# A second router by chunks: regions of rows per expert, sent as each chunk is routed, and shared tail tiles behind the experts

## The chip, the cores and the metric

One core of one Trainium2 chip runs the kernel. Its engines are named as in the profile: PE (TensorE, with PEld its weight loads), DVE (VectorE), ACT (ScalarE), POOL (GpSimd), SP (SyncE), and 16 DMA engines. The metric is the device time of one execution in microseconds; the median of three executions of the kernel before is 945.3 us (945.02 to 947.12).

## The reference, cut to what matters

Two layers over 2048 tokens of width 256, float32. The first layer (causal attention with 16 heads, and a mixture of 16 experts, two per token) is not touched, but for zeros that are written beside it. The second:

```python
xn = _layernorm(x)
x = x + _L1_attn_ref(xn, W, b) + _L1_ffn_ref(xn, ...)

# attention without a softmax, from sums over the tokens
q, k, v = split(xn @ W + b)
attn = q / norm(q, axis=1) * sum(k / norm(k, axis=1) * v, axis=1)

# 4 of 16 experts per token, and a shared expert
probs = softmax(xt @ w_router)
top_w, top_i = top_k(probs, 4);  top_w = top_w / sum(top_w)
moe_out = sum over the 4 of top_w * (silu(xt @ we1[e]) * (xt @ we3[e])) @ we2[e]
shared = silu(xt @ ws1) * (xt @ ws3) @ ws2
out = shared / 5 + moe_out * 4 / 5
```

## The kernel before, in words

Tokens lie in 16 tiles of 128 (T), in four chunks of four tiles (C, TC). Each engine has its own program in each of three blocks; semaphores order them, and a block ends when all engines have ended theirs.

`stage_first` is the first layer: an order of steps planned in advance (`attention_plan`) for PE, ACT, DVE and POOL. SP's program in it also writes zeros over `xd1`, the scratch for the second layer's dispatched rows, in five transfers (line 723).

`stage_second` has two parts. Its front is a loop over tiles (DVE's turns from line 1690, PE's from 1815): PE transposes the attention's output, DVE divides by the softmax sums, PE transposes back and multiplies by `w_o` (1840), DVE adds to the residual (1695) and takes norm statistics. After every four tiles DVE makes the variance (1702), ACT its root (1635), DVE the normalized rows `xn` one chunk behind. `turn_and_score(c)` on PE (1799) transposes a chunk of `xn`, ACT copies it to `xt` (1642; two tiles ahead of the next chunk's root, two behind it), and PE computes router logits (1811). The calls for chunks 0, 1 and 2 stand in PE's turns 9, 13 and 17; the last follows the loop. Then PE forms the Gram product of `xn` (1851), from which the norms and sums of the linear attention follow, runs 16 units of the shared expert's first layer (`shared`, 1863 and 1869; ACT's silu, DVE's `gated`, 1739), with the norms' work after 13 of them, and multiplies ten "tail" tiles: the shared expert's second layer and `q`'s projection (1910, 1912). DVE adds them in pairs (1793). In the meantime DVE routes all 16 tiles at once: softmax (1721 to 1727), four best per token and their indices (`route_best`, 130), then `route` (140): masks, ranks by two matmuls on PE (`route_ranks`, after Gram tile 8), a scan of counts, a slot for each row so that an expert's rows lie together and padded to 128, and the table `tile_e` with each tile's expert. `route` hands each of the four choices to POOL, which sends 64 times 128 rows of 1032 bytes to `xd1` by indirect DMA (1625). A row carries its own place for the way back.

`stage_experts` runs 79 tiles of 128 dispatched rows through their experts, in a loop unrolled 16 times (`rolled`, 1268): SP loads a tile at `j * 128` (1356), PE transposes it (1475), multiplies by both first matrices (1484), transposes the product (1492), multiplies by the second (1499); ACT and DVE copy and gate; POOL computes the rows' home (1448) and scatters the result by indirect DMA (1454). PE's program loads 20 registers with expert numbers at the head of each body. Then PE multiplies the last six tail tiles (1509), SP and ACT each fetch eight tiles' four rows per token (1363, 1390), and the weighted sums are made by DVE for tiles 0 to 7 (1430) and by PE for tiles 8 to 15, with diagonal matrices of weights that DVE has built (1422, 1517); DVE adds what PE has summed (1438), and SP stores tile by tile (1366).

## Time and profile before

| | |
|---|---|
| median of three executions | 945.3 us |
| profiled execution, its own time | 946.62 us |
| its span | 944.6 us, granted clock 0.964 |
| busy in the span | PE 864.8 (92%), DVE 642.2 (68%), ACT 417.2 (44%), POOL 422.0 (45%) |
| DMA moved | 113.6 MB, mean 120 GB/s |

```profile
PE   5887789899999999999999977789998879999997
DVE  5589799888788888887888952575714514444466
POOL 3323065515544336435353464000477826766640
PEclk9998599999999999999999999896999989999999
DMA  9643956421561312911110122640122225555549
```

Each digit is the busy share of a fortieth of the span (23.6 us) in tenths, for PEclk the clock granted to TensorE in tenths of full speed. The attention fills the first 25 slices. The second layer's block begins with slice 26 (about 598 us), the expert loop with slice 33 (about 770 us), and the last slice and a half is the fetch and the sums. POOL idles in slices 27 and 28, and the dispatch of rows lies in slices 29 to 33.

### The profile page before, as it was taken

To read this page: it belongs to the slowest core of one execution; us is meant where nothing else is said; L and a number is where in the kernel's file an instruction comes from. 1 tells how busy PE (TensorE), PEld (TensorE's weight loads), DVE (VectorE), ACT (ScalarE), POOL (GpSimd) and SP (SyncE) were. 2 spreads that over 40 slices of the span, in tenths; PEclk is the share of its full clock that TensorE was granted. 3 is DMA by queue.
4 is the path that set the end of the run, shared out by engine and by line. 5 is a ranking of instruction groups with operands and counts; after the bars stand their busy time and mean duration, and the time that the engine had idled before them with its cause. 6 is when DMAs were issued, how large, how long until landed. Compare 5 with 4: busy or idle time off the path is not lost. (4 is left out here: it accounts for less than half of the span.)

```text
span 944.6 us, 16014 instructions
## 1 busy us (share of the span) xinstructions
PE 864.8 (92%) x4827; PEld 468.3 (50%) x4828; DVE 642.2 (68%) x1528; ACT 417.2 (44%) x739; POOL 422.0 (45%) x719
## 2 busy tenths in 40 slices
PE   5887789899999999999999977789998879999997
PEld 3533223334444444444444321567544667787886
DVE  5589799888788888887888952575714514444466
ACT  3633145465666666665666667222112013333310
POOL 3323065515544336435353464000477826766640
PEclk9998599999999999999999999896999989999999
DMA  9643956421561312911110122640122225555549
GB/s 330 210 131 120 217 113 174 143 45 34 123 176 61 115 46 78 204 45 52 43 50 23 57 66 65 234 162 1 51 100 97 81 76 147 156 152 155 153 164 359
DMA packets 71393, 113.60 MB, mean 120 GB/s; under 512 B 12054, under 2 KB 55318, under 8 KB 70806
## 3 DMA queue, kind: packets, MB, share of 16 engines
q1 hardware_dynamic: 50774, 57.76, 22.2%
q0 software_dynamic: 16000, 45.70, 14.3%
q10 hardware_dynamic: 4544, 9.21, 3.2%
q8 instruction: 38, 0.62, 0.3%
q14 instruction: 37, 0.30, 0.1%
HBM read 58.19 MB, written 54.15 MB: 119 GB/s over the span
## 5 line engine op out<-in xcount | busy, mean ns | idle before, releaser
L1069 DVE TENSOR_REDUCE part_max<-ps_row 128x1 f32<-128x512 f32 (+3 forms) x560 | 353.5, 670 | 69.8 <-PE ps_row L1223 40.5
L939 ACT ACTIVATE probs<-ps_st 128x1024 f32<-128x1024 f32 (+3 forms) x320 | 278.5, 897 | 201.1 <-PE ps_st L1202 199.9
L1127 PE MATMUL ps_o<-probs,v_all 128*17 128x512 f32 (+3 forms) x1280 | 148.5, 536 | 14.4 <-ACT probs L939 8.6
L1223 PE MATMUL ps_row<-ks,qs 96*128 96x512 bf16 (+3 forms) x320 | 109.6, 376 | 12.2 <-DVE part_max L1069 9.0
L1223 PE MATMUL ps_row<-xt_ks,qs 96*128 96x512 bf16 (+3 forms) x320 | 103.1, 350 | 1.0 <-DVE part_max L1069 0.5
L1454 POOL DMA_INDIRECT yd<-moe_ys,moe_home x79 | 78.1, 989 | 44.2 <-POOL moe_home L1448 28.8
L1202 PE MATMUL ps_st<-qs,ks 99*128 99x512 bf16 (+3 forms) x320 | 88.8, 360 | 3.7 <-DMA qs<-max_parts 3.5
L1202 PE MATMUL ps_st<-qs,xt_ks 99*128 99x512 bf16 (+3 forms) x320 | 82.7, 348 | 2.1 <-ACT probs L939 1.3
L1484 PE MATMUL moe_ps_h<-w,moe_xs_t 128*128 x316 | 83.3, 387 | 0.0
L1223 PEld LDWEIGHTS ps_row<-ks,qs 96*128 96x128 bf16 x320 | 31.9, 100 | 94.3 <-DVE part_max L1069 57.3
L1401 DVE TENSOR_TENSOR moe_hid<-moe_ps_h,moe_act 128x128 f32<-128x128 f32 x79 | 23.0, 291 | 76.8 <-ACT moe_act L1384 76.8
L1625 POOL DMA_INDIRECT xd<-xn,slot x64 | 65.9, 1030 | 18.7 <-issue 9.8
L811 POOL TENSOR_SCALAR_AFFINE_SELECT probs<-probs 128x256 f32<-128x256 f32 x128 | 52.4, 416 | 48.9 <-ACT probs L939 47.5
L821 POOL TENSOR_SCALAR moe_h_tanh<-moe_h_tanh 128x128 f32<-128x128 f32 x47 | 24.9, 529 | 96.9 <-ACT moe_h_copy L951 96.6
L1223 PEld LDWEIGHTS ps_row<-xt_ks,qs 96*128 96x128 bf16 x320 | 30.8, 96 | 74.2 <-DVE part_max L1069 40.7
L1377 ACT COPY moe_xs_t<-moe_ps_x 128x256 f32<-128x256 f32 x79 | 29.4, 373 | 76.1 <-PE moe_ps_x L1475 75.8
L1484 PEld LDWEIGHTS moe_ps_h<-w,moe_xs_t 128*128 128x128 f32 x316 | 55.0, 194 | 4.6
L799 POOL DMA_INDIRECT xd<-o_t,slot x32 | 31.3, 977 | 47.3 <-ACT probs L939 42.8
L1127 PEld LDWEIGHTS ps_o<-probs,v_all 128*17 128x17 f32 x1280 | 21.8, 95 | 61.1 <-ACT probs L939 37.1
L1226 PE MATMUL ps_row<-mask,ident 128*128 128x128 bf16 x256 | 50.7, 225 | 0.0
L1202 PEld LDWEIGHTS ps_st<-qs,xt_ks 99*128 99x128 bf16 x320 | 27.4, 98 | 41.9 <-ACT probs L939 21.7
L1499 PE MATMUL moe_ps_y<-we,moe_hid_t 128*128 x158 | 47.2, 382 | 0.0
(266 smaller groups left out, 1329.4 us busy)
## 6 DMA issues: line engine op xcount, KB each, us to landing
moe_xs<-xd SPq DMA_DIRECT2D x79, 129.0 KB, 2.1
xd<-zeros SPq DMA_DIRECT2D x4, 2064.0 KB, 10.3
qk_parts<-probs SPq DMA_DIRECT2D x16, 384.0 KB, 3.3
qs<-qk_parts SPq DMA_DIRECT2D x96, 64.0 KB, 2.5
moe_xs<-xd POOLq DMA_DIRECT2D x47, 128.0 KB, 2.4
yd<-moe_ys POOLq DMA_DIRECT2D x47, 128.0 KB, 2.1
xd<-zeros POOLq DMA_DIRECT2D x2, 2048.0 KB, 15.6
moe_w<-in_w ACTq DMA_DIRECT2D x2, 2048.0 KB, 20.1
```

The lines of the kernel that those rows point to most:

```text
L799: pool.indirect_dma_start(out=m.xd0, out_offset=bass.IndirectOffsetOnAxis(m.r["slot"][:, choice, i:i + 1], 0), in_=m.xn[:, i, :], in_offse ...
L811: pool.affine_select(out=corner, in_=corner, compare_op=ALU.is_ge, fill=keep, base=0, pattern=[[0, 2], [1, P]], channel_multiplier=-1).the ...
L939: act.activation(probs[:, at % NPB, :, off:CH], ps_st[at % 2][:, :, off:CH], ACT.Exp, scale=HD ** -0.5).then_inc(exp_done, 1)
L1069: dve.tensor_reduce(part_max[reduced % 2][:, h:h + k, i, j:j + 1], bank[:, 0:k * w].rearrange("p (h w) -> p h w", h=k), AX_X, ALU.max).the ...
L1127: mm = pe.matmul(ps_o[32 * q:32 * q + HD + 1, off:CH], m.v_all[:, k, g * HG + q, :], probs[:, (at + q // 2) % NPB, q % 2, off:CH], start=F ...
L1202: mm = pe.matmul(ps_st[n % 2][:, h, off:CH], ks[g % 2][:, q, k * P:(k + 1) * P], qs[c][:, q, off:CH], start=True, stop=True)
L1223: mm = pe.matmul(cols, qs[c][0:KROWS, h, i * P:(i + 1) * P], ks[g % 2][0:KROWS, h, j * CH:j * CH + w], start=True, stop=(j < c))
L1226: mm = pe.matmul(cols[:, w - P:w], m.ident16[:, :], m.mask16[:, :], start=False, stop=True)
L1454: pool.indirect_dma_start(out=yd, out_offset=bass.IndirectOffsetOnAxis(home[:, k:k + 1].bitcast(U32), 0), in_=ys[:, k % U, :], in_offset=N ...
L1484: mm = pe.matmul(ps_h[b][:, :], xs_t[:, b, k, :], w1[:, k, bass.ds(e, 1), :], start=(k == 0), stop=(k == KH - 1))
L1499: pe.matmul(ps_y[b][:, :], hid_t[:, b, :], w2[:, bass.ds(e, 1), :], start=True, stop=True).then_inc(y_done, 1)
L1625: pool.indirect_dma_start(out=m.xd1, in_=xn[:, i, :], in_offset=None, out_offset=bass.IndirectOffsetOnAxis(r["slot"][:, k, i:i + 1], 0)).t ...
```

## The change

It alters where the second layer routes, where rows go, and who makes the last sums.

- **Routing by chunks.** The logits, the softmax, the best four, the masks, the ranks and the slots are computed for a chunk of four tiles at a time (`chunk_ranks`, `chunk_best`, `chunk_slots`). Those of chunks 0 and 1 stand between DVE's turns in the loop over tiles: scores of 0 after turn 10, best of 0 after 12, slots of 0 after 13, scores of 1 after 14, best of 1 after 16; the rest follows the loop. PE multiplies for the ranks of chunks 0 and 1 behind `turn_and_score(1)` and `(2)`, for 2 and 3 behind Gram tiles 0 and 5. ACT's exp is four steps.
- **A region per expert.** Expert `e` owns rows from `e * CAP` on, `CAP` = 2048 + 128, so a row's slot needs only the counts of the chunks before. `xd1` grows to 16 * 2176 + 128 rows. POOL sends a chunk's 16 tiles-of-choices as its slots are ready, waiting for the landing of a half's rows before it overwrites the home column.
- **Pads.** Zeros are written over one tile only (the last); when all is routed, SP copies it behind the end of each region, 16 transfers.
- **A table of first rows** (`tile_row`), made by `tile_tables` beside `tile_e` in pieces between gated units. SP loads 16 of its entries into registers for every 16 tiles.
- **Tail.** `TAIL_FIRST` 10 becomes 2: fourteen tail tiles are multiplied behind the experts. DVE makes all weighted sums, two tiles at a time, and SP stores pairs. Diagonals and PE's sums are gone.

```diff
-        if "home" not in r:
-            dve.tensor_copy(r["slot"][:, k, :], r["slotf"][:, k, :]).then_inc(slots_ready, 1)
-        else:
-            ...
+        dve.tensor_copy(r["slot"][:, k, :], r["slotf"][:, k, :]).then_inc(slots_ready, 1)
...
+def chunk_ranks(pe, r, c, masks_ready):
+    pe.wait_ge(masks_ready, c + 1)
+    flat = r["any16"][:, c * TC:(c + 1) * TC, :].rearrange("p i e -> p (i e)")
+    pe.matmul(r["ps_ranks"][c], r["before16"][:, :], flat, start=True, stop=True)
+    return pe.matmul(r["ps_counts"][c], r["ones16"][:, :], flat, start=True, stop=True)
+
+def chunk_best(dve, step, r, c, scores, masks_ready):
+    tiles = range(c * TC, (c + 1) * TC)
+    cs = slice(c * TC, (c + 1) * TC)
+    route_best(dve, step, r, scores, tiles)
+    step.then(dve.tensor_copy(r["argf"][:, cs, 0:TOP1], r["arg"][:, cs, 0:TOP1]))
+    step.then(dve.tensor_tensor(r["hots"][c], r["argf"][:, cs, 0:TOP1].rearrange("p i k -> p k i").unsqueeze(
+        3).to_broadcast([P, TOP1, TC, E]), r["iota_e"].unsqueeze(1).to_broadcast([P, TOP1, TC, E]), ALU.is_equal))
+    ...
+        dve.tensor_reduce(r["any16"][:, cs, :], r["hots"][c].rearrange("p k i e -> p i e k"), AX_X,
+                          ALU.add).then_inc(masks_ready, 1)
+
+def chunk_slots(dve, step, r, c, ranks_ready, slots_ready):
+    given, start, place = r["given"][:, c, :, :], r["start"][:, c, :, :], r["place"]
+    dve.wait_ge(ranks_ready, c + 1)
+    step.then(dve.tensor_copy(given[:, :, 1:TC + 1], r["ps_counts"][c].rearrange("p (i e) -> p e i", e=E)))
+    step.then(dve.tensor_tensor_scan(start.rearrange("p e i -> p (e i)"), r["inside"],
+                                     given.rearrange("p e i -> p (e i)"), 0.0, ALU.mult, ALU.add))
+    step(dve.tensor_tensor(place, r["ps_ranks"][c].rearrange("p (i e) -> p i e", e=E),
+                           start[:, :, 0:TC].rearrange("p e i -> p i e"), ALU.add))
+    if c + 1 < C:
+        step(dve.tensor_copy(r["given"][:, c + 1, :, 0], start[:, :, TC]))
+    step.sync()
+    step.then(dve.tensor_tensor(r["placed"], r["hots"][c], place.unsqueeze(1).to_broadcast([P, TOP1, TC, E]),
+                                ALU.mult))
+    cs = slice(c * TC, (c + 1) * TC)
+    step.then(dve.tensor_reduce(r["slotf"][:, :, cs], r["placed"], AX_X, ALU.add))
+    dve.tensor_copy(r["slot"][:, :, cs], r["slotf"][:, :, cs]).then_inc(slots_ready, 1)
...
 stage_first, SP
-                    if c >= 2 and at_tile < NT1:
-                        clear(sp, m, m.xd1, at_tile, min(NT1, at_tile + CLEAR), m.cleared[1])
-                        at_tile += CLEAR
+                    if (g, c) == (1, 0):
+                        clear(sp, m, m.xd1, E * CAP // P, E * CAP // P + 1, m.cleared[1])
...
 stage_experts
-                    sp.dma_start(xs[:, u % U, :], xd[bass.ds(j * P, P), :]).then_inc(x_in[u % U], 16)
-            rolled(sp, 0, tiles, BODY, tick)
+                    sp.dma_start(xs[:, u % U, :], xd[bass.ds(first_rows[u], P), :]).then_inc(x_in[u % U], 16)
+            rolled(sp, 0, tiles, BODY, tick, load_rows)
...
+            for n in range(T // 2):
+                pair = (2 * n, 2 * n + 1)
+                dve.wait_ge(fetched[n], 32)
                 for k in range(top):
-                    step(dve.tensor_scalar(diag[:, t, k, :], m.ident[:, :], m.r["weight"][:, i, k:k + 1], float(TOP1 + 1),
-                                           ALU.mult, ALU.mult))
...
+                    for i in pair:
+                        step(dve.scalar_tensor_tensor(m.x[:, i, :], yg[i][:, k, :], m.r["weight"][:, i, k:k + 1],
+                                                      m.x[:, i, :], ALU.mult, ALU.add))
+                    step.sync()
+                if 2 * n < TAIL_FIRST:
+                    dve.sem_inc(finished, 1)
                 else:
+                    dve.wait_ge(tail_done, n + 1 - TAIL_FIRST // 2)
+                    both = m.x[:, 2 * n:2 * n + 2, :]
+                    dve.scalar_tensor_tensor(both, ps_tail[n].rearrange("p (i d) -> p i d", d=D), 1.0 / (TOP1 + 1), both,
                                              ALU.mult, ALU.add).then_inc(finished, 1)
...
-                    pool.tensor_tensor(home[:, j:j + 1], xs[:, j % U, D + 1:XW].bitcast(I32), ring[:, j % U:j % U + 1],
-                                       ALU.add).then_inc(home_ready, 1)
+                    pool.tensor_scalar(home[:, j:j + 1], xs[:, j % U, D + 1:XW], ring[:, j % U:j % U + 1], None,
+                                       ALU.max).then_inc(home_ready, 1)
...
-TAIL_FIRST = 10
+TAIL_FIRST = 2
-GRAM_FIRST = 8
+RANKS_IN_GRAM = {0: 2, 5: 3}
...
 stage_second, SP
+            sp.wait_ge(m.cleared[1], 16)
+            sp.wait_ge(pads_ready, 1)
+            pads = nc.values_load_multi_w_load_instructions(
+                pad_row[0:1, 0:E], engines=[mybir.EngineType.SP], ...)[1]
+            for first in pads:
+                sp.dma_start(m.xd1[bass.ds(first, P), :], m.xd1[E * CAP:E * CAP + P, :]).then_inc(padded, 16)
+            sp.wait_ge(padded, 16 * E)
...
 stage_second, POOL
+            for c in range(C):
+                pool.wait_ge(slots_ready, c + 1)
+                for k in range(TOP1):
+                    for half in range(2):
+                        i = c * TC + 2 * half
+                        if k:
+                            pool.wait_ge(dispatched[half], 32 * (c * TOP1 + k))
+                        step.then(pool.tensor_copy(xn[:, i:i + 2, DP:XW], home[:, k, i:i + 2].unsqueeze(2)))
+                        for i in (i, i + 1):
+                            pool.indirect_dma_start(out=m.xd1, in_=xn[:, i, :], in_offset=None,
+                                                    out_offset=bass.IndirectOffsetOnAxis(r["slot"][:, k, i:i + 1], 0)
+                                                    ).then_inc(dispatched[half], 16)
...
 stage_second, ACT and DVE
+                if i in (10, 14):
+                    exp_of(i // TC - 2)
...
+                if i in (10, 14):
+                    scores_of(i // TC - 2)
+                if i in (12, 16):
+                    best_of(i // TC - 3)
+                if i == 13:
+                    chunk_slots(dve, step, r, 0, ranks_ready, slots_ready)
```

## Rows read from the trace of the kernel before

**Rows 1.** Windows: length, busy PE, PEld, DVE, ACT, POOL (counts), clock, DMA share, GB/s.

```profile
300.00:400.00 100.00, 99.58 (x693) 45.67 (x695) 84.11 (x160) 62.04 (x99) 49.14 (x106) 1.00 0.44 110
...
650.00:652.00 2.00, 2.00 (x12) 2.00 (x11) 0.00 (x0) 1.73 (x3) 0.00 (x0) 0.50 0.00 0
...
908.00:945.00 37.00, 31.59 (x141) 26.32 (x141) 25.22 (x75) 0.00 (x0) 3.35 (x4) 0.99 0.78 298
```

**Rows 2.** Chain of waits that ended last: start, duration, what.

```profile
918.30 20.46 DMA we<-yd
```

**Rows 3.** Timeline of PE, second layer: start, duration, line, what [idle before <- releaser].

```profile
633.53 0.63 PE L1820 MATMUL ps_ab<-ident,o_t 128*128 128x128 f32 x4
...
648.34 2.25 PE L1806 MATMUL ps_t<-ident,xn 128*128 128x128 f32 x8
...
653.65 9.87 PE L1851 MATMUL ps_gram<-xn 128*128 128x257 f32 x36
...
679.08 1.98 PE L1869 MATMUL ps_ab<-xt,ws 128*128 128x512 f32 x4 [0.36 <-DVE o_t L1739]
...
743.04 1.89 PE L1910 MATMUL ps_gram<-ws,o_t 128*128 128x256 f32 x8
...
745.63 1.89 PE L1910 MATMUL ps_gram<-ws,o_t 128*128 128x256 f32 x8
```

**Rows 4.** Timeline of DVE, second layer: turns 14 and 17, first and last tail sums.

```profile
634.20 0.26 DVE L1684 RECIPROCAL rec<-ps_ab 128x16 f32<-128x16 f32 x1 [2.15 <-PE ps_ab L1820]
...
643.38 0.42 DVE L1695 TENSOR_TENSOR x_res<-ps_o,x_res 128x256 f32<-128x256 f32 x1 [1.56 <-PE ps_o L1840]
...
745.90 0.69 DVE L1793 SCALAR_TENSOR_TENSOR x_res<-ps_gram,x_res 128x512 f32<-128x512 f32 x1 [1.34 <-PE ps_gram L1912]
...
766.55 0.69 DVE L1793 SCALAR_TENSOR_TENSOR x_res<-ps_t,x_res 128x512 f32<-128x512 f32 x1 [4.49 <-PE ps_t L1912]
```

**Rows 5.** Timeline of POOL, the dispatch: its first, longest and last send.

```profile
670.84 1.00 POOL L1625 DMA_INDIRECT xd<-xn,slot  x1 [0.36 <-POOL xn L1623]
...
741.04 4.37 POOL L1625 DMA_INDIRECT xd<-xn,slot  x1 [0.31 <-issue]
...
760.74 0.97 POOL L1625 DMA_INDIRECT xd<-xn,slot  x1 [0.31 <-issue]
```

**Rows 6.** Groups by line, DVE, 595 to 670: busy us, mean ns, idle before.

```profile
L133 DVE MAX8 best<-scores 128x8 f32<-128x16 f32 x16 | 1.3, 160 | 0.0
...
L210 DVE TENSOR_TENSOR masks<-masks,count 128x256 f32<-128x256 f32 x2 | 1.2, 593 | 0.0
...
L181 DVE TENSOR_TENSOR_SCAN before<-within,count 128x256 f32<-128x256 f32 x1 | 0.7, 691 | 0.0
...
L161 DVE TENSOR_REDUCE top_sum<-best 128x16 f32<-128x64 f32 x1 | 0.2, 213 | 0.0
```

**Rows 7.** Timeline of ACT, second layer: a root in the front, a table load.

```profile
632.08 0.20 ACT L1635 ACTIVATE std<-var 128x4 f32<-128x4 f32 x1 [0.59 <-DVE var L1702]
...
651.02 1.28 ACT L1661 ACT_TABLE_LOAD   x1
```

**Rows 8.** Page: transfers (KB each, us to landing); groups by line: POOL's home step.

```profile
moe_xs<-xd SPq DMA_DIRECT2D x79, 129.0 KB, 2.1
...
L1448 POOL TENSOR_TENSOR moe_home<-moe_xs,moe_ring 128x1 int32<-128x1 int32 x79 | 15.4, 195 | 5.5 <-DMA moe_xs<-xd 3.1
```

**Rows 9.** Waits, 769 to 912: total us, times, longest.

```profile
PE moe_ps_x L1475 <- issue: 4.2, 4, 1.2
```

**Rows 10.** Timeline from 900 and page group: first and last sum, tail, mean.

```profile
909.41 1.89 PE L1509 MATMUL moe_ps_x<-ws,o_t 128*128 128x256 f32 x8
...
919.43 2.05 DVE L1430 SCALAR_TENSOR_TENSOR x_res<-moe_yg,weight,x_res 128x256 f32<-128x256 f32 x4 [3.13 <-DMA w<-yd]
...
940.74 0.75 DVE L1438 SCALAR_TENSOR_TENSOR x_res<-moe_ps_g,x_res 128x256 f32<-128x256 f32 x2
...
L1430 DVE SCALAR_TENSOR_TENSOR x_res<-moe_yg,weight,x_res 128x256 f32<-128x256 f32 x32 | 15.5, 483 | 4.8 <-DMA w<-yd 3.9
```

More of the change, by code:

```diff
@@ L35 @@
 XW = D + 2
+CAP = S + P
 YRING = 4
 IN_RANGE = "the routing counts from zero and takes the minimum with E - 1"
+ROW_IN_RANGE = "a region holds every token and P rows more, and the minimum with E * CAP is taken"
 EPS = 1e-5
@@ new lines, in choice_weights, with region_ends @@
+def choice_weights(dve, step, r, top, factor):
+    best = r["best"]
+    step.then(dve.tensor_reduce(r["sum"][:, :], best[:, :, 0:top], AX_X, ALU.add))
+    step.then(dve.reciprocal(r["sum"][:, :], r["sum"][:, :]))
+    step(dve.scalar_tensor_tensor(r["weight"][:, :, 0:top], best[:, :, 0:top], factor,
+                                  r["sum"][:, :].unsqueeze(2).to_broadcast([P, T, top]), ALU.mult, ALU.mult))
+def region_ends(dve, r, pads_ready):
+    dve.tensor_copy(r["pad_row"][:, :], r["start"][0:1, C - 1, :, TC]).then_inc(pads_ready, 1)
@@ L1285, in rolled, with shared_tail @@
         tick(j, j % unroll)
+def shared_tail(pe, m, bank, i):
+    cols = bank[:, i % 2 * D:(i % 2 + 1) * D]
+    for s in range(HS // P):
+        pe.matmul(cols, m.hid_s[:, s, i * P:(i + 1) * P], m.ws2[:, s, :], start=(s == 0), stop=False)
+    for k in range(KH):
+        mm = pe.matmul(cols, m.xt2[:, k, i * P:(i + 1) * P], m.wq[:, k, :], start=False, stop=(k == KH - 1))
+    return mm
 def stage_experts(nc, m, out):
@@ L1536, in stage_second @@
         home = l.sb("home", [P, TOP1, T], I32)
-        place = l.sb("place", [P, TOP1, T], I32)
+        given, start = l.sb("given", [P, C, E, TC + 1]), l.sb("start", [P, C, E, TC + 1])
+        inside, place = l.sb("inside", [P, E, TC + 1]), l.sb("place", [P, TC, E])
+        pad_row = l.sb("pad_row", [1, E], I32)
         w = l.sb("w_attn", [P, KH, 3 * D])
@@ L1636, in root_of, with exp_of @@
                                ACT.Sqrt).then_inc(std_ready, 1)
+            def exp_of(c):
+                cs = slice(c * TC, (c + 1) * TC)
+                act.wait_ge(logit_ready, c + 1)
+                act.activation(scores[:, cs, :], scores[:, cs, :], ACT.Exp).then_inc(exp_ready, 1)
             def copy_turned(c, tiles):
@@ L1659, in _ @@
             copy_turned(C - 1, range(TC))
-            act.wait_ge(logit_ready, 1)
-            act.activation(scores[:, :, :], scores[:, :, :], ACT.Exp).then_inc(exp_ready, 1)
+            exp_of(C - 2)
+            exp_of(C - 1)
             act.wait_ge(gram_done, 1)
@@ L1740, in gated @@
                                   ALU.mult).then_inc(hid_ready, 1)
-            for n in range(BEFORE_NORMS):
+            gated(0)
+            gated(1)
+            choice_weights(dve, step, r, TOP1, TOP1 / (TOP1 + 1))
+            tables = tile_tables(dve, step, r, NT1)
+            for n in range(2, BEFORE_NORMS):
+                next(tables, None)
                 gated(n)
```

201 lines of the change are left out of this document (103 added, 98 removed).

## The prediction

> **What bounds the kernel now.** I read busy times by stage first: PE is 99.6% busy in the attention, and in the last 37 us the DMA engines (0.78), PE and DVE share the load [rows 1]; in the expert loop PE stands only 4.2 us, for its own registers [rows 9]. The chain of waits then says how the end is made: PE up to the last expert tile, 20.46 us of fetching routed rows, DVE's last sums [rows 2]. Last the timelines. In the second layer's front (598 to 654) PE, DVE and ACT hand work to each other; from 653.65 PE runs nearly alone: the Gram product, the shared units, then ten tail tiles, 2.59 us apart [rows 3]; DVE adds their last pair at 766.55 [rows 4]. POOL sends rows beside this from 670.84 to 761.71 [rows 5]: 90.9 us for 64 sends, so POOL would hold the stage by itself if PE's part alone got shorter. The reader is to see three places: the front, the tail tiles, the end.
>
> **1. Eight tail tiles leave the stage.** Only the first pair stays, which DVE adds at 745.90; the fifth was added at 766.55 [rows 4]: 20.65 us less. The early routing also frees DVE, for which PE waited 0.36 us at 679.08 [rows 3]: -0.36. What is late next is POOL. It gets chunk 0 at about 639 (below); 64 sends at 90.9 - 3.4 (one send took 4.37 instead of 0.97) = 87.5 us end near 727, or 730 with such a send, against a stage end near 752. New are 24 waits for rows sent four sends before instead of sixteen; a pair of sends takes 2.7 us and the other half's pair lies between, so I take no wait. Until each costs 0.9 us the cover of 22 us hides them: 0.
>
> **2. The router by chunks costs time in the front.** Before, it lay in DVE's block beside the Gram product. Now scores of two chunks, the best of two and the slots of one stand inside the loop over tiles. Prices from the full-size steps [rows 6]: 64 elements take 0.21 us, 256 of a product 0.59, the scan of 256 takes 0.69, 16 maxima 1.3, and a dependent step starts 0.04 later. Scores of a chunk: two of 64 elements, 0.38. Best: three small steps 0.72, four maxima 0.40, four index searches (two instructions each) 0.66, a copy 0.22, a comparison and a sum over 256 elements 0.79: 2.8 us. Slots: copy 0.25, scan of 80 elements 0.36, two small steps 0.33, product 0.63, sum 0.46, cast 0.09: 2.1 us.
> Followed through the trace: scores(0) delays DVE's turn 11 by 0.4. best(0) stands ahead of turn 13, and turn 13 makes the variance that ACT's root at 632.08 waits for [rows 7]. Behind this root in ACT's queue stand the copies of two turned tiles, behind those on PE the logits of chunk 1 and the transposes at 633.53 [rows 3]. So PE is 3.2 us late there, and 0.2 more by the two rank matmuls. slots(0) waits for these and stands 2.1 us ahead of turn 14, which began at 634.20 [rows 4] and now begins near 639.3: +5.1. From there to turn 17 (643.38) scores(1) and best(1) add 3.2 and DVE's waits there, the longer of 1.56 us [rows 4], give back 1.9: +6.4. The last turn-and-score on PE (648.34, [rows 3]) had its input 0.9 us early; it now starts +5.6, and so does the Gram product: 659.2 instead of 653.65.
> Exp by chunks makes ACT load a table four times more, 1.28 us each [rows 7]. Three of the loads end before their input is there. The one ahead of exp(2) follows ACT's last copies and puts the masks of chunk 2 at about 661.5, where PE asks for them after its first Gram tile: +0.3, and +0.2 for two more pairs of rank matmuls. Sum of the part: 5.6 + 0.3 + 0.2 = +6.1. Bounds: 11.7 if nothing is absorbed (8.5 of steps added and 3.2 for the queue behind the root), 2 if PE's clock helps as in (a). I take 6.1, since the order of the queues leaves only the waits named to absorb.
> For the table loads the Trainium skill (ScalarE: Activation LUTs, What ACT_TABLE_LOAD costs) gives 2.66 us a switch, with a drain of 1.38 behind the load. In this trace an activation follows its load at once where its input is there. By the page exp(2) would be 1.4 us later and the time 944.6.
>
> **3. Tables, pads, clears.** The tile table and the new table of first rows are cut into pieces of 1.3 to 1.9 us between gated units, where DVE idles 2.7 us each time: 0, and 8 if that cover were gone. SP's 16 pad copies of 129 KB start near 670; a transfer of that size lands in 2.1 us [rows 8], so even one after the other they are done by 705: 0. The clears of 10 MB leave the attention, where PE was full while they ran (300 to 400 in [rows 1]): 0, with -1 as the other end. The one clear that stays is the size of one load: 0.
>
> **4. Expert loop.** SP has to load 16 registers before its first transfer. Nearest is PE, which stands those 4.2 us at the heads of four bodies, loading 20 each: 16/20 x 1.0 = +0.8, once. The later loads fall where SP waits between transfers (one each 1.63 us, 0.33 to issue): 0; 3.3 if none were hidden. POOL's maximum takes the place of an addition on 128x1 that took 195 ns [rows 8]. POOL's send begins 0.4 us behind this step, though in the stage before a send begins 0.28 behind a copy: it has some 0.12 us a tile to spare. 0, and +4 if the new form takes 0.17 us longer (0.05 x 79).
>
> **5. The end.** DVE summed eight tiles while PE summed eight with diagonal weights: 919.43 to 941.49 = 22.06 us, the pace of the fetches [rows 10]. Now DVE sums sixteen. A product-sum is 483 ns [rows 10], the next independent one starts 0.09 us before its end, a dependent one 0.04 after it. A pair of tiles is four times 0.394 + 0.483 + 0.04, 3.66 us. Seven pairs also add the shared tail, 0.69 us for 512 columns (as at 766.55), 0.61 of it in line: 4.27. In all 3.66 + 7 x 4.27 + 0.1 = 33.65 us: +11.6. The first pair lands as before, since the same transfers go first; the others land 2.8 us apart and are hidden. PE's fourteen tail tiles take 14 x 2.59 = 36.3 us from the end of its last expert tile, on the old times 909.41 to 945.7 [rows 10], and DVE asks for the last at 952: hidden by 6 us. The 32 diagonal weights (6.35 us on DVE) lay beside the fetch: leaving them out brings 0. The last store has 256 KB instead of 128: +0.4, between 0 and 1.
>
> **Sum.** -20.65 - 0.36 + 6.1 + 0.8 + 11.6 + 0.4 = -2.1 us. The profiled execution took 946.6 us for a span of 944.6; it would take 944.5 for 942.5. It stood 1.3 above the median of three, 945.3, and against that median I forecast 943.2.
>
> **The rivals.**
> (a) The front costs less. PE's clock is at 0.50 of its full speed (1.2 GHz) from 641 to 657 now, as at 650 in [rows 1]. If it stays at 2.4 the last turn-and-score takes 3.1 us as the first ones did instead of 5.3, and the Gram product 1.8 less: 939.2. Against it: the clock fell after PE had idled 1.95 and 0.89 us within 5 us, and it will idle more.
> (b) The other side: the front costs more. Behind best(0) PE idles some 3.4 us in one piece. If its clock falls to 1.2 GHz there, chunk 1's logits come 0.9 us later and turn 16's product 1.0, and a Gram product that is slow for 4 us more than now takes 2 us longer, with DVE's small steps longer beside POOL's sends (up to 0.19 us each at 672 to 674) by 1: the front costs 11 and the time is 948.1. It turns slower once the front costs over 10.1 us. For it speaks the length of the gap, against it that most of PE's work there waits for DVE anyway.
> (c) POOL's new form or SP's register loads hold the expert loop: +4, 947.2. Against it the spare times in 4.
> (d) The change does not do what it says: POOL still ends the stage, because each pair waits for its landing. At 1.5 us a wait it is 36 us later, at 766 instead of 752: 957. DVE can slow its sends: that at 741.04 took 4.37 us [rows 5] while DVE did one addition of 4.42 us with both operands in SBUF. The Trainium skill (SBUF — State Buffer, SBUF: two separate sides) says that such a DVE step and a GpSimd step exclude each other; the trace agrees in this one place. The other such DVE steps take under 0.75 us.
>
> **How the numbers follow.** About 0.2% (1.9 us) is what a measurement of this kernel can tell from no change. Chances: as worked out 0.5 (941 to 945.5, of it 0.3 below 943.4 and 0.2 above), (a) 0.17, (b) 0.17 (0.03 of it within 0.2%), (c) 0.12 (0.04 within), (d) 0.04. Faster 0.3 + 0.17 = 0.47, same 0.27, slower 0.26. The range reaches from (a) to (b): 939.2 to 948.2.
>
> **What would show it.** DVE's turn 14 about 5 us later, POOL's first send near 639.5, the Gram product near 659, the first tail matmul near 746, a stage ended by DVE near 752 with POOL done by 730, PE's first expert tile near 757, 1.63 us a tile, and in the end DVE without a wait for 33 us with PE's tail done before it. It would be wrong by a front that costs more than 10 or less than 3 us, by POOL ending the stage, by another pace in the loop, or by DVE waiting in the end.

## The result, and the profile after

The changed kernel takes 942.1 us (median of 11 runs, 940.3 to 947.7) where the kernel before takes 946.35 beside it (11 runs, 945.0 to 948.9): a ratio of 0.9958, with a 95% interval of 0.9945 to 0.9971. By the ratio that is 4.0 us less (4.2 between the two medians), where 2.1 were forecast, and 942.1 where 943.2 was. Here and below a ratio leaves out the runs that took over 1.5% longer than the fastest of the same kernel; beside the result there were none. The profiled execution has a span of 939.6 us (its own time is 941.45), against 944.6 before: 5.0 less.

To see where the 5.0 us lie I cut both traces at the same six places and count the first three from the second layer's first transpose on PE (597.97 before, 595.96 after):

| us | before | after | difference | forecast |
|---|---|---|---|---|
| attention and all ahead of it | 597.97 | 595.96 | -2.0 | 0 |
| Gram product starts | 55.68 | 62.60 | +6.9 | +5.6 |
| DVE's last addition of the stage ends | 169.27 | 155.25 | -14.0 | -14.9 |
| POOL's next block starts | 171.40 | 156.10 | -15.3 | -14.9 |
| from there to the first expert transpose | 2.04 | 2.83 | +0.8 | +0.8 |
| to PE's first tail matmul (the expert loop) | 138.00 | 138.77 | +0.8 | 0 |
| to DVE's first sum of routed rows | 10.02 | 9.69 | -0.3 | 0 |
| DVE's sums, first to last | 22.06 | 33.70 | +11.6 | +11.6 |
| from there to the end of the span | 3.11 | 2.55 | -0.6 | +0.4 |

(The Gram row and the DVE row lie inside the one for POOL's block and are not added.) The sum is -2.0 - 15.3 + 0.8 + 0.8 - 0.3 + 11.6 - 0.6 = -5.0.

The front on DVE, from the timeline of the kernel after; columns: start, duration, engine, line, operation, tiles, shapes, count, and in brackets the idle time before it and what ended it:

```profile
634.04 0.21 ACT L1725 ACTIVATE std<-var 128x4 f32<-128x4 f32 x1 [2.33 <-DVE var L1818]
```

```profile
633.84 0.17 DVE L1818 TENSOR_SCALAR var<-mv 128x4 f32<-128x4 f32 x1
636.02 0.23 DVE L262 COPY given<-ps_l 128x64 f32<-128x64 f32 x1 [2.02 <-PE ps_l L242]
...
638.06 0.26 DVE L1781 RECIPROCAL rec<-ps_ab 128x16 f32<-128x16 f32 x1
...
649.02 0.42 DVE L1811 TENSOR_TENSOR x_res<-ps_o,x_res 128x256 f32<-128x256 f32 x1
...
657.50 0.22 DVE L1797 TENSOR_REDUCE peak<-scores 128x4 f32<-128x64 f32 x1 [1.71 <-ACT scores L1731]
```

ACT's root now stands at 634.04, DVE still idles 2.02 us behind its variance and then makes slots (2.1 us) ahead of turn 14, which starts at 638.06 instead of 634.20 [rows 4]. Turn 17's addition (649.02) comes 7.65 us later than before, counted from the stage's start. The 1.71 us at 657.50 are the table load ahead of the third exponential; they are nearly hidden, since PE needs the masks only after its first Gram tile: DVE has them at 660.64, and PE's rank product starts at 660.70, 0.1 us behind that tile. PE's side of the same stretch, and the stage's end:

```profile
658.56 2.06 PE L1976 MATMUL ps_gram<-xn 128*128 128x257 f32 x4
...
675.06 1.45 PE L1988 MATMUL ps_ab<-xt,ws 128*128 128x512 f32 x3
...
745.00 1.97 PE L1366 MATMUL ps_gram<-ws,o_t 128*128 128x256 f32 x8 [0.94 <-DVE o_t L1856]
...
754.89 1.46 PE L1557 MATMUL moe_ps_x<-ident,moe_xs 128*128 128x128 f32 x4 [4.48 <-DMA moe_xs<-xd]
```

The first tail matmul follows at 745.00 (before 740.38) and only one pair of tiles stands before the experts. POOL, from its timeline: first and last send, and its next block.

```profile
639.05 1.01 POOL L1715 DMA_INDIRECT xd<-xn,slot  x1 [0.59 <-POOL xn L1713]
...
728.42 0.97 POOL L1715 DMA_INDIRECT xd<-xn,slot  x1 [0.30 <-issue]
752.06 0.13 POOL L1525 IOTA moe_ring_i<- 128x4 int32 x1 [22.67 <-POOLq L1606]
```

The sends end 22.67 us before the next block, which starts 0.85 us after DVE's last addition (750.52 and 0.69 long). In the trace of before the same row reads otherwise:

```profile
760.74 0.97 POOL L1625 DMA_INDIRECT xd<-xn,slot  x1 [0.31 <-issue]
769.37 0.13 POOL L1444 IOTA moe_ring<- 128x4 int32 x1 [7.66 <-POOLq L1532]
```

There POOL's next block started 7.66 us after its last send and 2.13 us after DVE's last addition [rows 4]. So POOL, not DVE, had the last word in that stage; the experiment with late routing below shows the same 7.6 us. The instructions at the end of the block, which the profile does not count as busy, say so directly (line, engine, operation, duration in ns, start in us):

```profile
L1532 POOLq COMPARE_BRANCH  x1: 46/46/46, 763.3 to 763.3; - x1
L1532 POOLq DRAIN  x1: 5382/5382/5382, 763.7 to 763.7; - x1
L1532 DVEq DRAIN  x1: 17/17/17, 767.5 to 767.5; - x1
L1532 SPq EVENT_SEMAPHORE  x1: 17/17/17, 769.3 to 769.3; - x1
```

POOL's program waits at its end for the landing of its rows. At 763.3, 2.6 us after the last send began, it is past that wait; then a drain instruction, which stands at the end of each engine's block, keeps POOL from 763.7 to 769.1. DVE's took 0.02 us and was over at 767.5, and the other engines go on at 769.3, when POOL's is over. After the change the same drain (5.30 us) begins at 731.2, 15 us before DVE is done.

The end, from the timelines of DVE and PE:

```profile
903.35 1.80 DVE L1511 SCALAR_TENSOR_TENSOR x_res<-moe_yg,weight,x_res 128x256 f32<-128x256 f32 x4 [9.06 <-DMA moe_yg<-yd]
...
932.71 3.62 DVE L1511 SCALAR_TENSOR_TENSOR x_res<-we,weight,x_res 128x256 f32<-128x256 f32 x8
936.36 0.69 DVE L1519 SCALAR_TENSOR_TENSOR x_res<-moe_ps_y,x_res 128x512 f32<-128x512 f32 x1
```

```profile
929.06 1.03 PE L1368 MATMUL moe_ps_y<-wq,xt 128*128 128x256 f32 x4
```

DVE works from 903.35 to 937.05 without a wait; PE's last tail tile is done at 930.1, 6.3 us before DVE asks for it.

### The profile page after: what moved, and what is told of

The parts are those of the page before. It is cut to its first block and busy times, and to the rows that moved or that the text cites. A ratio compares the mean times of both kernels' runs of the same rounds, so it can differ in the third digit from the quotient of the medians.

```text
span 939.6 us, 16080 instructions
## 1 busy us (share of the span) xinstructions
PE 849.5 (90%) x4769; PEld 455.7 (48%) x4770; DVE 654.9 (70%) x1551; ACT 422.8 (45%) x746; POOL 433.9 (46%) x720
## 5 line engine op out<-in xcount | busy, mean ns | idle before, releaser
L1536 POOL DMA_INDIRECT yd<-moe_ys,moe_home x79 | 82.5, 1045 | 31.4 <-POOL moe_home L1530 16.6
L1715 POOL DMA_INDIRECT xd<-xn,slot x64 | 63.5, 992 | 19.0 <-issue 9.7
```

Source lines behind the costliest of these rows:

```text
L1536: pool.indirect_dma_start(out=yd, out_offset=bass.IndirectOffsetOnAxis(home[:, k:k + 1].bitcast(U32), 0), in_=ys[:, k % U, :], in_offset=N ...
L1715: pool.indirect_dma_start(out=m.xd1, in_=xn[:, i, :], in_offset=None, out_offset=bass.IndirectOffsetOnAxis(r["slot"][:, k, i:i + 1], 0)).t ...
```

## The experiments

**Four parts taken back or moved, on one chip.** The kernel before took 946.35 us beside them (17 runs), as beside the result.

**1. The clears put back.**

```
+                    if c >= 2 and at_tile < NT1:
+                        clear(sp, m, m.unused, at_tile, min(NT1, at_tile + CLEAR), m.cleared[1])
+                        at_tile += CLEAR
```

> The changed kernel with the five clears of 10 MB put back at their old places in the attention, onto rows in DRAM that nothing reads, and with the wait for them on SP before the pads. The changed kernel stands 4.0 us below the kernel before (942.1 against 946.35), and in its profile the attention ended 2.0 us earlier. Theory A (the clears held the attention up): 2.0 us are given back, the ratio to the kernel before goes from 0.9958 to 0.998 and the second layer's first transpose moves from 595.96 back to 598. Theory B (the 2.0 us are the phase of PE's clock after one wait at 67 us, before any clear starts): the time stays at 942.1, ratio 0.9958, and the start of the second layer differs from 596 only if the matmuls at 67 us are slow again.

Measured: 943.85 us (12 runs), ratio 0.9977 (0.9963 to 0.9992). The ratio lies at the 0.998 of theory A and not at the 0.9958 of theory B, but its interval touches that of the change (0.9945 to 0.9971), so the times alone leave anything from nothing to over 3 us to the clears. The profile speaks for theory B: with the clears, the second layer began at 595.60.

```profile
66.75 1.88 PE L1246 MATMUL ps_st<-xt_ks,moe_ys 128*128 128x512 f32 x4
...
595.60 1.94 PE L1947 MATMUL ps_ab<-ident,o_t 128*128 128x128 f32 x8 [3.42 <-PEq L666]
```

The four products at 66.75 took 1.88 us, as after (66.84), where the profiled execution of before took 3.54 at 66.92: that difference stands 70 us ahead of the first clear. And the five profiled executions of this chip and of the result that have the changed kernel's attention (one of them with the clears) began the second layer at 595.60, 595.96, 597.33, 601.02 and 602.66. A difference of 2 us there, between one execution and another, says nothing of the change. All fourteen profiles sort by the four products: where they took 1.88 us the second layer began at 595.60 to 596.26 in five, with and without the clears, and at 598.54 in the sixth; where they were slower it began at 597.33 to 602.66 in eight, with both kernels. A cost of the clears of up to 2 us in the medians is not excluded.

**2. All ten tail tiles back in the stage.**

```
-TAIL_FIRST = 2
+TAIL_FIRST = 10
```

> The changed kernel with all ten tail tiles back in the stage before the experts, as in the kernel before. Theory: the stage ends 20.65 us later with DVE's last addition near 771.2, POOL done 40 us before it; the end loses four paired additions of 0.61 us (-2.4) and PE has 20.7 us less to do there. Sum +18.2: 960.3 us, 1.4% above the kernel before. Rival (the moved tiles cost again in the end, by contention of PE with DVE's sums or with the fetches): then taking them out of the end gives back more than 2.4 us, DVE's 33.7 us from first to last sum fall below 31, and the time is under 958.

Measured: 961.31 us, ratio 1.0171 (1.0158 to 1.0184), 19 us above the changed kernel. In the profile the stage ends 20.57 us later after its start, and DVE's sums last 31.78 us instead of 33.70: -1.92 for four additions, 0.48 each and not 0.61. The addition's 0.61 us show here too (950.18 to 950.79), but a pair of tiles without one then takes 3.78 us instead of 3.66, with 0.15 us of wait before the next pair. No contention shows: the moved tiles cost in the end what DVE's additions cost and nothing else.

**3. Routing behind the loop.** Scores, best choices and slots of chunks 0 and 1 follow DVE's last normalization; their ranks go into the Gram product.

```
-                if i in (10, 14):
-                    scores_of(i // TC - 2)
-                if i in (12, 16):
-                    best_of(i // TC - 3)
-                if i == 13:
-                    chunk_slots(dve, step, r, 0, ranks_ready, slots_ready)
...
-RANKS_IN_GRAM = {0: 2, 5: 3}
+RANKS_IN_GRAM = {1: (0, 1), 7: (2,), 12: (3,)}
```

> The changed kernel with the routing of chunks 0 and 1 (scores, best choices, slots, and ACT's exponentials) taken out of the loop over tiles and put behind it, their ranks on PE into the Gram product. Theory: the front gets its 6.6 us back: DVE's turn 14 at 632.2 instead of 638.06, the Gram product from 651.7 instead of 658.56. But POOL then has its first slots only near 656, and 64 sends take 90.3 us: POOL ends near 747 instead of 729.4 and, with its last landing, ends the stage at 748.5 in place of DVE, which would be done at 744 to 746. So of 6.6 us only some 2 arrive: 940.2. Rival A (the front's loss is not made by these steps but by the clock of PE): the Gram product still starts after 656 and the time is 945 or more, since POOL starts later. Rival B (POOL's sends get quicker when they lie apart from the front): the whole 6.6 us arrive, 935.5.

Measured: 951.12 us, ratio 1.0053 (1.0040 to 1.0066): 9 us slower than the change, where 2 less were expected; the expectation failed. In its profiled execution the second layer began at 602.66:

```profile
658.37 3.77 PE L1974 MATMUL ps_gram<-xn 128*128 128x257 f32 x8
...
669.63 0.20 PE L241 MATMUL ps_l<-any,before 128*128 128x64 bf16 x1 [1.10 <-DVE any L254]
...
675.11 0.20 PE L241 MATMUL ps_o<-any,before 128*128 128x64 bf16 x1 [0.83 <-DVE any L254]
```

```profile
665.42 1.01 POOL L1715 DMA_INDIRECT xd<-xn,slot  x1 [0.59 <-POOL xn L1713]
...
747.65 4.87 POOL L1715 DMA_INDIRECT xd<-xn,slot  x1 [0.30 <-issue]
...
759.70 0.97 POOL L1715 DMA_INDIRECT xd<-xn,slot  x1 [0.30 <-issue]
768.29 0.13 POOL L1525 IOTA moe_ring_i<- 128x4 int32 x1 [7.62 <-POOLq L1606]
```

```profile
747.26 4.42 DVE L1910 TENSOR_TENSOR x_res<-x_res,bq 128x4096 f32<-128x4096 f32 x1
...
753.01 0.69 DVE L1915 SCALAR_TENSOR_TENSOR x_res<-ps_gram,x_res 128x512 f32<-128x512 f32 x1 [1.34 <-PE ps_gram L1368]
```

The theory holds for the front: the Gram product starts 55.71 us after the stage's start, as before (55.68), so all 6.9 us come from these steps (with their exponentials and rank products), and none from PE's clock by itself (what the clock adds comes with the waits that they make). Of the 6.9 us, 4.2 reach DVE's last addition (151.04 us after the stage's start instead of 155.25): inside the Gram product PE now waits 1.10 and 0.83 us for masks, as its two rank rows show. What I had wrong is POOL. Its first send goes 62.76 after the stage's start; 64 sends last 95.3 us, one of them 4.87 beside DVE's addition of 4.42 over all tiles (the pair of [rows 5] again); and its next block starts 7.62 us after the last, 14.6 us after DVE's last addition at 753.70. I had put the first send some 2 us too early and the sends 5 us too short, and allowed 1.5 us for the landing where the landing and the drain take 7.6. Early routing is therefore worth far more than the trace of DVE and PE shows: it is what lets POOL be done in time.

**4. Two tiles' sums on PE.**

```
+                        for k in range(top):
+                            mm = pe.matmul(ps_tail[n][:, i % 2 * D:(i % 2 + 1) * D], diag[:, i - T + ON_PE, k, :],
+                                           yg[i][:, k, :], start=False, stop=(k == top - 1))
```

> The changed kernel with the routed sums of the last two tiles moved to PE, as products with diagonal weights into the banks of their shared tail; DVE makes the 8 diagonals (1.6 us) while the fetch runs. Theory (DVE alone sets the end, PE waits there 6.3 us): DVE's sums shrink by one pair, 3.66 us, to 30.0; PE's last pair gets 2 x 1.73 us longer and ends near 933.6, where DVE asks for it at 932.7: -3.66 + 0.9 = -2.8 to -3.3 us, 939 us. Rival (the end is already held by the fetch of rows or by the store): the last rows land late, PE waits for them, and the gain is under 1 us.

Measured: 941.43 us, ratio 0.9945 (0.9933 to 0.9958). DVE's sums last 30.49 us instead of 33.70, with one wait of 0.35 for PE:

```profile
938.03 0.69 DVE L1527 SCALAR_TENSOR_TENSOR x_res<-moe_ps_y,x_res 128x512 f32<-128x512 f32 x1 [0.35 <-PE moe_ps_y L1607]
```

In the trace it is the -3.2 us that were expected: DVE alone set the end, and neither fetch nor store did. (The profiled execution itself is 1.7 us longer than that of the change, because its attention took 5.1 us more.) In the medians only 0.7 us arrive, and the intervals overlap; five runs against the scatter seen in experiment 1 don't settle the rest. It stands below the kernel before with its whole interval; below the changed kernel it is not shown.

**Eight more runs, on other chips.** For them the kernel before itself took 978 to 981 us, and nothing in their times can be held against 946.35: in the stage before the experts PE, DVE and ACT stood for tens of us while POOL sent rows (last section). I read from them only what lies ahead of these stalls or behind them.

**5. One tail pair left out of the kernel before** (twice; the output lacks the shared expert of tiles 8 and 9).

```
-*ps_t, *ps_ab][0:TAIL_FIRST // 2]
+*ps_t, *ps_ab][0:TAIL_FIRST // 2 - 1]
```

> The kernel before with one pair of tail tiles (tiles 8 and 9) left out of the stage before the experts, and out of the kernel altogether, so that the output lacks the shared expert of these 256 rows: PE 5.17 us and DVE one addition less. Theory A (as forecast: DVE's last addition ends the stage): the next block starts 5.2 us earlier, 941.2 us. Theory B (from the traces: in the kernel before, POOL's next block starts 7.66 us after its last send ends, in the changed one it starts 0.85 us after DVE's last addition with POOL long done; so POOL's block with its sends in flight, ended at 169.3 + 2.1 after the start of the second layer's stage, held the stage before): the next block starts only 0 to 0.3 us earlier, at 171.1 to 171.4 after the stage's start, and the time stays at 946.3, within 0.1%. POOL's 7.7 us stay.

> The kernel before with one pair of tail tiles (8 and 9) left out altogether, once more, on a chip where no engine is starved beside POOL's sends, if it is given one. Expectations as before: theory A (DVE's last addition ended the stage before) 5.2 us less; theory B (POOL's block, 7.66 us after its last send, held it): the next block starts 171.1 to 171.4 us after the stage's start as in the kernel before, and the time is unchanged within 0.1%.

Measured: 972.25 us, 0.9921 (0.9888 to 0.9953), and 974.99, 0.9941 (0.9926 to 0.9956), beside 978.38 and 980.84. The 6 us that went look like theory A, but say nothing on the question: in both, the stalls brought DVE's end to 197.2 and 200.1 us after the stage's start, long behind POOL's block, so that DVE's tiles had to count there. What the two traces do give is the other price: where DVE ends this kernel's stage, POOL's next block starts 0.53 us behind DVE's last addition, in both. In the kernel before it started 2.13 us behind, so POOL held that stage 1.6 us beyond what DVE needed; together with the drain rows above this is what theory B rests on. Its forecast for the time was not tested.

**6. Routing steps where DVE waits** (twice).

```
+                    if i == 14:
+                        scores_of(1)
...
+                if i == 13:
+                    best_of(0)
+                if i == 15:
+                    chunk_slots(dve, step, r, 0, ranks_ready, slots_ready)
...
+            best_of(1)
```

> The changed kernel with the routing steps moved to where DVE waits in the front: best choices of chunk 0 behind turn 13's variance (before it, the next wait was 2.15 us), scores of chunk 1 ahead of turn 14's addition, slots of chunk 0 behind turn 15, best choices of chunk 1 behind the loop. Theory (the front's loss of 6.9 us is made by steps ahead of ACT's root and by too little idle time to take them): counted from the second layer's first transpose, the Gram product starts at 59.3 instead of 62.6, POOL's first send goes at 46 to 49 instead of 43.1 and its block would be done at 146 (91 us of sends and 7.6), so DVE still ends the stage, at 152 instead of 155.25: -3.3 us, 938.8 us. Rival (the front's cost is PE's slow clock, not the place of the steps): the Gram product starts at 61.5 or later and the gain is under 1 us.

> The changed kernel with the routing steps moved to where DVE waits, once more. Up to the Gram product the first look showed what was forecast: it started 59.77 us after the stage's start instead of 62.60, POOL's first send at 47.41 instead of 43.09. Theory: DVE ends the stage 2.8 to 3.3 us earlier, near 152.2, POOL's block would be done at 145.5, and the time is 939.0 (ratio to the kernel before 0.9925). Rival (the gain is lost again before the stage ends, in the Gram product, whose ranks now come later): DVE ends the stage at 154 or later and the ratio is 0.995 or more.

Measured ahead of the stalls: the Gram product starts at 59.77 and 59.76 instead of 62.60, POOL's first send at 47.41 and 47.39. So 2.8 of the 6.9 us of the front were a matter of place. Four steps moved at once, so no one of them has its share measured, but turn 14 shows where most of it comes from: it starts 37.96 us after the stage's start, where the changed kernel has 42.10 and the kernel before 36.23, with the best choices of chunk 0 right ahead of it and behind the variance that ACT's root waits for:

```profile
630.65 0.17 DVE L1820 TENSOR_SCALAR var<-mv 128x4 f32<-128x4 f32 x1
...
633.78 0.25 DVE L1781 RECIPROCAL rec<-ps_ab 128x16 f32<-128x16 f32 x1
```

The times (ratios 1.0174 and 1.0185 to the kernel before) are those of the stalls: 206 and 213 us to the next block. Whether the 2.8 us reach the end of the stage on a chip without them was not seen.

**7. The same, and no tail pair before the experts** (twice), **and the changed kernel with that alone.**

```
-TAIL_FIRST = 2
+TAIL_FIRST = 0
```

> As the run with the moved routing steps, and the last pair of tail tiles moved behind the experts too. Theory: the stage loses another 5.2 us of PE (DVE's last step is then its addition over all tiles or the end of PE's shared units, near 147 after the stage's start), POOL's block end at 146 comes within 1 us of it; in the end DVE adds one pair more (+0.5) and PE's 16 tail tiles take 41.6 us from the last expert tile, while DVE asks for the last pair at 43.4 + 0.5: hidden by 2. Sum -3.3 - 5.2 + 0.5 = -8.0 against the changed kernel: 934.1 us. Rival (POOL's block holds the stage): the next block starts 7.6 us after the last send whatever DVE does, and the gain is 1 to 4 us smaller.

> As the run beside it, and the last pair of tail tiles moved behind the experts too. Theory: the next block starts near 148.0 after the stage's start instead of 156.1 (POOL's block is done at 145.5), the end costs 0.5 us more; against the changed kernel -2.9 - 5.2 + 0.5 = -7.6 us: 934.5, ratio 0.9875. Rival: in the end PE's 16 tail tiles (41.5 us) are late for DVE, and 2 us or more of the gain are lost there.

> The changed kernel with the last pair of tail tiles moved behind the experts too (none is left in the stage before them). Theory: POOL's block is done 15 us before DVE ends the stage, so the whole 5.17 us of PE leave it, as 20.6 us did for four pairs; the end costs 0.5 us more, since DVE adds one pair more (34.20 instead of 33.70 us of sums, as seen in the kernel with the same end) and PE's 16 tail tiles still end 2.3 us before DVE's last addition: -4.7 us, 937.5 us or 0.991 of the kernel before. Rival (POOL's block comes to hold the stage): under 2 us less. On a chip on which the kernel before takes 978 to 981 us, where the engines' instructions come late while POOL sends rows, the changed kernel's sends start 34 us earlier and lie over more of the other engines' work: there the ratio is 1.01 to 1.02, by some 50 us of stall in the stage instead of 30.

Measured: 992.37 us (ratio 1.0124, 1.0064 to 1.0183) and 995.87 (1.0170, 1.0146 to 1.0193) with the moved steps; 986.46 without. Of these last six runs (963.2 to 999.7) three took 995 or more and the ratio of 0.9914 (0.9861 to 0.9968) is that of the other three; the median of all six is 5.6 us above the kernel before. The 1.01 to 1.02 that was expected for such a chip did not come, and the scatter is too wide to say more. (That expectation has the sends start 34 us earlier; by the traces it is 29.8.) Behind the stalls the end did what was expected: in the second run with the moved steps DVE's sums lasted 34.20 us (+0.50) and PE's last tail tile ended at 982.91, 2.31 us before DVE did (985.22).

That the changed kernel with `TAIL_FIRST = 0` would take some 937 us where the change takes 942 is worked out from these numbers, not measured.

**8. POOL's step for the row numbers twice.**

```
+                    pool.tensor_scalar(home2[:, j:j + 1], xs[:, j % U, D + 1:XW], ring[:, j % U:j % U + 1], None, ALU.max)
```

> The changed kernel with POOL's maximum for the row numbers of an expert tile issued twice, the second into a tile that nothing reads (0.30 us more on POOL in each of 79 tiles). Theory A (POOL has less to spare than this, 0.03 to 0.12 us a tile): the loop becomes POOL's, 0.18 to 0.27 us a tile longer, +14 to +21 us, 956 to 963. Theory B (the wait between POOL's two steps of a tile, 0.23 us, takes most of it in): 0 to +5 us. If it is A, the loop of the changed kernel ran at the edge of POOL, and the new form's 0.1 us a tile was the most it could have borne.

Measured: 1006.39 us beside 978.38. In the loop, POOL is without a gap:

```profile
881.19 1.05 POOL L1538 DMA_INDIRECT yd<-moe_ys,moe_home  x1 [0.16 <-POOL moe_home L1532]
882.29 0.30 POOL L1530 TENSOR_SCALAR moe_home<-moe_xs,moe_ring 128x1 int32<-128x1 f32 x1
882.56 0.27 POOL L1532 TENSOR_SCALAR moe_home<-moe_xs,moe_ring 128x1 int32<-128x1 f32 x1
882.99 1.05 POOL L1538 DMA_INDIRECT yd<-moe_ys,moe_home  x1 [0.16 <-POOL moe_home L1532]
```

A tile takes 1.80 us. Less the second step's 0.27 that is 1.53 for POOL alone, against PE's 1.63: 0.10 us a tile are left in the changed kernel. The loop lasts 146.1 us, 8 more than 138 and not 79 times 0.17, which is 13; that PE's 4.2 us for its registers now hide behind POOL would account for about as much, but was not shown. Theory A has the bound right and its price (14 to 21 us) too high; theory B's (up to 5) is too low.

## Why the prediction was right, point by point

**1. Tail tiles.** The 20.65 us left the stage; putting them back brought 20.57. PE's 0.36 went too. But POOL was costed by its sends alone (ending near 727; they ended at 729.4). Its cover was put at 22 us and is 15.0, because its block lasts 7.6 us beyond the last send; and the same 7.6 us had held the end of the stage before, so that the next block started 2.13 us behind DVE's last addition and now starts 0.85 behind it: 1.3 us that the forecast lacks. (The hold itself was 1.6 us, by experiment 5's 0.53; the changed kernel's own start behind DVE is 0.3 longer.) These 1.3 us are the mis-sized term: I read the stage's end off DVE's last addition, when the row to read was what the next block's first instruction waited for. The 64 sends took 90.3 us where 87.5 were forecast. Of these 2.8 us, 1.2 are two waits for landing (24 were taken to cost nothing) and 1.0 is one send of 1.95 us; they lie under the cover, and rival (d) did not come.

**2. The front.** +5.6 and +0.5 were forecast; the Gram product came +6.9 later and the first shared unit +7.1. The order of queues was as told (root, copies, logits, ranks, slots, turn 14), and experiment 3 puts all of it down to the routing steps. The sizes were short by 1.0: best(0) took 3.05 us instead of 2.8 (its comparison and sum 0.96 instead of 0.79); and DVE's addition of turn 10, ahead of the first routing step, came 25.39 us after the stage's start instead of 24.87 (25.4 to 25.6 in experiments 1, 2 and 6, but 24.51 in 3 and 24.40 in 4), which no step explains. The wait at turn 17, 1.56 us [rows 4], was taken in as forecast. The price of the third exponential's table was right: 1.28 us, with the activation 0.01 us behind it,

```profile
655.92 1.28 ACT L1731 ACT_TABLE_LOAD   x1
657.21 0.26 ACT L1731 ACTIVATE scores<-scores 128x64 f32<-128x64 f32 x1
```

and the 2.66 us of the Trainium skill (ScalarE: Activation LUTs, What ACT_TABLE_LOAD costs) do not show here. PE's clock did not help (a), and it hurt a little as (b) has it. It was at 0.50, which is 1.2 GHz, from 635.2 to 638.6, from 645.5 to 648.9 and from 652.3 to 662.5, where before it was from 640.3 to 657.3. The first of these stretches is new: behind best(0) PE idled 2.86 us, then it began the last logits of chunk 1, and its clock fell 0.7 us into them:

```profile
630.74 0.96 PE L1933 MATMUL ps_l<-w_router,xt 128*128 128x16 f32 x8
...
634.56 1.32 PE L1933 MATMUL ps_l<-w_router,xt 128*128 128x16 f32 x8 [2.86 <-ACT xt L1737]
```

The same eight products took 0.96 us at full clock, so DVE, which waits for the ranks behind them, got its slots some 0.4 us later; in experiment 4, where the clock had fallen before them, they took 1.89, the 0.9 us of (b). This 0.4 is a part of the missing 1.0. The rest of (b) did not come: the Gram product ran at the slow clock for 4.0 us against 3.7 before, and lasted 16.5 us against 16.3.

**3. Tables, pads, clears.** The tables and the pads cost nothing. The -2.0 us of the attention in the profile lie within the scatter from one execution to another (experiment 1); whether the clears are worth up to 2 us in the medians stays open.

**4. The loop.** The registers cost +0.8 as forecast: 2.83 us from the block's start to the first transpose instead of 2.04, and 2.86 to 2.99 in experiments 1 to 4. The loop's +0.77 in the profile is not POOL's form: with the same form the first four experiments have 137.07, 136.76, 138.44 and 137.96 us against 138.00 before. The form costs 0.30 us instead of 0.195, inside what POOL had to spare, of which experiment 8 finds 0.10 us a tile left; rival (c) did not come.

**5. The end.** 33.70 us for 33.65, by the same pace; PE's tail was hidden by 6.3 us, as forecast. The larger store costs nothing that shows (2.55 us from DVE's end to the end of the span, before 3.11): -0.6 where +0.4 was forecast, and no run says why.

**Sum.** Counted from the stage's start the profile has -3.0, the forecast -2.1. The difference of -0.9 is -1.3 at POOL's block, +0.9 by the front, +0.8 and -0.3 in the loop and the fetch, -1.0 at the store. The timed runs have -4.0, with an interval of 2.7 to 5.2 less. The forecast of 2.1 less lies just outside it: the direction and the stated range (939.2 to 948.2) hold, but the size is half of what was measured, and part of its nearness to the profile is luck, since +0.9 in the front and +0.8 in the loop cancel most of -1.3 at POOL's block and -1.0 at the store. What makes the rest of the difference to the timed runs, scatter or up to 2 us for the clears, stays open.

## What to carry to other kernels

Read the end of a stage from what the next block's first instruction waited for on each engine, not from the last arithmetic: here POOL's block was done 7.6 us after its last send, more than 5 of them in the drain at the block's end. When a stage is bound by two chains that end within 2 us of each other, shortening one is worth no more than these 2 us until the other starts earlier; here the early routing cost 7 us on one chain and bought 30 on the other. And count a moved step from where the queue behind it waits: experiment 6 gave back 2.8 of the front's 6.9 us without taking any step out.

## What the runs showed of the hardware

**POOL's block outlasts its last indirect send** by 7.66 us (before) and 7.62 us (experiment 3), though among the sends the waits for the send four before came to 1.2 us in all (experiment 3). The landing is the smaller part: POOL is past its wait for it 2.5 to 2.7 us after the last send began. The larger part is the drain at the end of its block, 5.38 us in the three profiles of the kernel before's form and 5.30 in those of the changed one, with or without stalls, where DVE's takes 0.02. It is not a matter of rows under way: at the end of the attention, where POOL's last instructions were masks (L811, the last ended at 593.99) and its last row transfer had begun 7.6 us before, its drain took 4.21 us,

```profile
L590 POOLq DRAIN  x1: 4214/4214/4214, 593.5 to 593.5; - x1
```

and there too the next block (597.94) began right behind it and not behind the other engines, of which ACT was the last at 595.2. What the drain waits for the runs don't show.

**A POOL send stands while DVE runs a step with both operands in SBUF:** 4.87 us for a send that began 0.39 us into a DVE step of 4.42 (experiment 3), and 4.37 for one that began 0.90 us into such a step [rows 5], where a send takes 0.97 otherwise; they ended 0.84 and 0.85 us behind the DVE step. The second pair's DVE row:

```profile
740.14 4.42 DVE L1788 TENSOR_TENSOR x_res<-x_res,bq 128x4096 f32<-128x4096 f32 x1
```

The Trainium skill (SBUF — State Buffer, SBUF: two separate sides) says that the two exclude each other, and both rows agree. That DVE waits for POOL in turn these rows don't show.

**On other chips the same program stalls beside POOL's sends.** The kernel before took 978 to 981 us there, 32 to 35 more. From experiment 8, two sends of POOL, then PE's rows around the same time:

```profile
718.70 0.97 POOL L1717 DMA_INDIRECT xd<-xn,slot  x1 [0.28 <-issue]
719.97 0.97 POOL L1717 DMA_INDIRECT xd<-xn,slot  x1 [0.30 <-issue]
```

```profile
719.06 1.01 PE L1990 MATMUL ps_t<-xt,ws 128*128 128x512 f32 x1 [1.87 <-issue]
721.86 1.01 PE L1990 MATMUL ps_t<-xt,ws 128*128 128x512 f32 x1 [1.79 <-issue]
724.77 1.01 PE L1990 MATMUL ps_t<-xt,ws 128*128 128x512 f32 x1 [1.90 <-issue]
...
740.25 1.88 PE L1990 MATMUL ps_t<-xt,ws 128*128 128x512 f32 x4
```

Each matmul waits nearly 2 us for nothing that the profile shows, at about the pace of one for two sends (2.8 to 2.9 us a matmul, some 2.7 for two sends), until the sends have ended (729.1); later four run in 1.88. In experiment 5's first kernel DVE stood 24.18 us and resumed 0.55 us after POOL's last send (758.58):

```profile
759.13 0.43 DVE L1759 TENSOR_SCALAR t<-bias_qkv 128x512 f32<-128x512 f32 x1 [24.18 <-remote]
```

That the engines' instructions arrive late is what it looks like; the Trainium skill (Runtime: NRT & Kernel Launch, Instruction fetch mechanics) says that each engine fetches its instructions in blocks through a DMA queue of its own, mostly hidden. The runs don't show the cause. With the early sends, more of PE's and DVE's work lies under them: the variants of the changed kernel took 1.2% to 2.8% more than the kernel before on two of these chips (the 2.8% with POOL's step doubled), and on the third the one without early tail tiles took from 1.8% less to 1.9% more. The changed kernel itself was not timed there; its gain of 0.4% is shown only where these stalls are absent.
